# The first attention of a two-layer block: a head's rotations at other steps

## The reference

```python
h = (x - mu) * rsqrt(var + LN_EPS) * ln_scale + ln_bias
c_q = h @ w_down_q.T                       # 2048 x 64
c_kv = h @ w_down_kv.T
q = (c_q @ w_up_q.T)                       # 16 heads of 64
k = (c_kv @ w_up_k.T)
v = (c_kv @ w_up_v.T)
q = _apply_rope_subspace(q, DR)            # e*cos - o*sin, e*sin + o*cos
k = _apply_rope_subspace(k, DR)
attn = softmax(einsum('bhqd,bhkd->bhqk', q, k) / 8)
out = einsum('bhqk,bhkd->bhqd', attn, v) @ w_out.T + residual
```

## Time and profile before

| | us |
|---|---|
| median of 3 runs | 2236.38 (2236.3 to 2242.65) |
| the profiled execution | 2237.01 |
| its span | 2235.1 |
| PE busy in the span | 2009.0 (90%) |
| DVE, ACT, POOL busy | 1694.8, 1625.8, 1633.9 |
| attention, step 0 to the last output product | 61.4 to 1297.1 |

### The profile page before, as it was taken

How to read it: one execution, slowest core, us unless ns; L and a number is a source line. 1 busy time by engine, 2 the same in 40 slices (tenths; PEclk the granted TensorE clock), 3 DMA queues, 4 the chain that set the end, 5 groups by cost and what they waited for, 6 DMA issues and landing times. The chain is left out here.

```text
span 2235.1 us, 60603 instructions
## 1 busy us (share of the span) xinstructions
PE 2009.0 (90%) x24318; PEld 1317.7 (59%) x24318; DVE 1694.8 (76%) x3487; ACT 1625.8 (73%) x3282; POOL 1633.9 (73%) x1036
## 2 busy tenths in 40 slices
PE   5899999999999999999999979976678787887888
PEld 2466666666666666666666646642456666666665
DVE  5677777777778777777777558978988898899624
ACT  3798898988988988988889936656656555574543
POOL 4799998999999999989989936626664334577700
PEclk8899999999999999999999989977889999899769
DMA  4000100010000001000100000111211111121201
GB/s 151 22 23 16 30 23 16 23 29 18 23 23 23 23 19 27 23 16 23 30 16 23 2 16 23 40 36 25 41 41 48 34 43 36 32 46 36 43 10 38
DMA packets 88224, 67.80 MB, mean 30 GB/s; under 512 B 41280, under 2 KB 78352, under 8 KB 87952
## 3 DMA queue, kind: packets, MB, share of 16 engines
q1 hardware_dynamic: 76432, 52.19, 9.1%
q0 software_dynamic: 11520, 11.82, 2.6%
HBM read 32.97 MB, written 1.61 MB: 15 GB/s over the span
## 5 line engine op out<-in xcount | busy, mean ns | idle before, releaser
L428 POOL TENSOR_TENSOR probs_lo<-probs,probs_hi 128x1024 f16<-128x1024 f32 x512 | 1077.0, 2134 | 87.3 <-ACT probs L477 86.2
L533 DVE TENSOR_REDUCE part_max<-aux 128x1 f32<-128x512 f32 x1024 | 690.0, 688 | 210.9 <-PE aux L608 206.0
L476 ACT ACTIVATE probs_hi<-scores 128x512 f16<-128x512 f32 x1024 | 632.8, 618 | 162.7 <-PE scores L641 149.0
L477 ACT ACTIVATE probs<-scores 128x512 f32<-128x512 f32 x1024 | 638.7, 624 | 0.0
L1732 POOL DMA_INDIRECT far<-key_table,placeT x320 | 328.6, 1027 | 236.8 <-issue 70.1
L655 PE MATMUL acc<-v,probs_hi 128*128 128x65 f16 x4096 | 445.9, 193 | 1.8 <-POOL probs_lo L428 1.8
L657 PE MATMUL acc<-v,probs_hi 128*128 128x64 f16 x4096 | 446.9, 195 | 0.0
L659 PE MATMUL acc<-v,probs_lo 128*128 128x65 f16 x4096 | 445.2, 193 | 0.0
L655 PEld LDWEIGHTS acc<-v,probs_hi 128*128 128x128 f16 x4096 | 383.0, 97 | 72.1 <-POOL probs_lo L428 2.1
L608 PE MATMUL aux<-k_a,q_a 128*128 128x512 f16 x1024 | 394.4, 386 | 32.4 <-issue 22.9
L657 PEld LDWEIGHTS acc<-v,probs_hi 128*128 128x128 f16 x4096 | 380.8, 97 | 68.9 <-issue 0.6
(11 more groups left out here) (335 smaller groups left out, 3619.1 us busy)
## 6 DMA issues: line engine op xcount, KB each, us to landing
q_a<-rope_high SPq DMA_DIRECT2D x128, 64.0 KB, 2.0
far<-key_table,placeT POOLq DMA_INDIRECT x360, 2.5
q_b<-rope_low SPq DMA_DIRECT2D x64, 64.0 KB, 2.0
k_b<-rope_high SPq DMA_DIRECT2D x64, 64.0 KB, 2.0
k_a<-rope_high SPq DMA_DIRECT2D x64, 64.0 KB, 2.1
k_a<-rope_low SPq DMA_DIRECT2D x64, 64.0 KB, 2.0
qT<-qT SPq DMA_DIRECT2D x16, 256.0 KB
queries<-places SPq DMA_DIRECT2D x7, 512.0 KB, 3.7
```

The costliest lines, as they stand in the source:

```text
L428: pool.tensor_tensor(probs_lo[:, slot], probs[:, wide], probs_hi[:, slot], ALU.subtract).then_inc(low_ready, 1)
L476: act.activation(probs_hi[:, slot, i], bank, ACT.Exp, scale=float(DH0) ** -0.5)
L477: act.activation(probs[:, wide, i], bank, ACT.Exp, scale=float(DH0) ** -0.5).then_inc(probs_ready, 1)
L533: dve.tensor_reduce(part_max[g % 2][:, n % QT, n // QT:n // QT + 1], bank, AX.X, ALU.max).then_inc(aux_free, 1)
```

## The change

`rope_at` returns other steps for heads 1 to 15: the first query pair 27 steps ahead of its head instead of 17, the key pairs 21 and 15 steps ahead instead of 30 and 23, and the second query pair 5 instead of 4. Head 0 keeps its own steps. In a head's own counting the next head's rotations now lie in steps 5 (first query pair), 11 and 17 (keys), and 27 (second query pair). ACT's copies, POOL's subtractions and SP's transfers move with them, since their places are worked out from the same function.

```diff
 def rope_at(kind, h, pair):
 
     if kind == "k":
-        return STEPS * (h - 1) + (2, 9)[pair] if h else -24 + pair
-    return STEPS * h - (17, 4)[pair] if h else (-25, 0)[pair]
+        return STEPS * h - (21, 15)[pair] if h else -24 + pair
+    return STEPS * h - (27, 5)[pair] if h else (-25, 0)[pair]
```

## The result

The changed kernel takes **2217.5 us** (median of six runs, 2214.95 to 2221.07). The kernel before, run beside it, took 2237.92 (2235.35 to 2242.65). The ratio is **0.9902, 95% interval 0.9884 to 0.992**: about 1% faster, against a forecast of 2214.5 in a range of 2208 to 2224. The profiled execution has a span of 2216.5 us, 18.6 less than before.

What follows compares the result with a forecast made beforehand. PE was taken to pace the first attention, with removable waits for the first queries' transfers in step 19. Terms -25.2 + 1.3 + 2 = -21.9 us, from the median 2236.4, gave 2214.5 us, range 2208 to 2224.

Steps and rivals of the forecast that it cites:

- The waits of step 19: Heads 1 to 14, PE before the second maximum product: all 14 waits go, 21.8 us, -25.2 us with half clock.
- Half clock behind two of the waits: Heads 3 and 11: half-speed stretches following PE's waits disappear, saving 3.4 us.
- Keys' margin: Step 23, second key pair's low halves: they land 1.5 us early in even heads, 2.9 in odd; no cost.
- The slower rival: Step 23: keys' subtraction two low halves later on POOL, trip misses its reader, 28 us more, 2242.5 us; chance 0.05.
- POOL and DVE: Whole heads and step 5: no added PE waits; at most 0.8 us for POOL and 1.4 us for DVE.
- Head 0's shade: Head 0, step 3: head 1's first key rotation leaves step 2, so PE's wait grows by 1.3 us.
- The residual addition: Head 0, around POOL's 4.53 us addition: moved rotations cost +2 us, within -1 to +2.5.
- The rival that PE is not the pacer: First attention: POOL needs PE's pause, which returns as waits for probs_lo; nothing gained, 2236 us; chance 0.06.

Runs made afterwards that it cites:

- second profile: The changed kernel run again without further edits, on the chip of the last comparison: 2217.71 us, 0.9907 of the kernel before.

## Why the prediction was right, and where it was not

**The waits of step 19: right.** Forecast -25.2 us for heads 1 to 14, measured -24.64. The reading as the tail of a trip, too long by 1.4 us, is shown by the lead of one step more and one step less. Half clock behind two of the waits went with them: the granted clock of heads 1 to 14 is 1.00, and even and odd heads last 73.51 and 76.23 us (73.5 and 76.3 forecast). The prediction called these two the longer waits; the longest of all, 2.52 us in head 10, had a granted clock of 1.00 in the 6 us behind it, so their length does not tell the two apart.

**Whose move removes them: too narrow.** The prediction gave all of it to the first queries' rotation, and priced the keys' move only for what it could cost. That step reckoned the trip against PE's work of before, and left out that the change puts a rotation of 1.30 us into just that stretch. The first queries' move alone is enough, and the keys' move without it brings 19.4 of the 24.6 us. The sum wasn't hurt, since either way the wait goes.

**Keys' margin, taken at nothing: right, but not as safe as written.** At best 1.37 us against 1.5. That is less than the scatter of a landing (median 2.1, at most 3.6 us in the changed kernel and 4.0 with one step less). It shows in the changed kernel in a few steps only, such as the 0.3 us in its list of waits. The slower rival was a real mechanism: two steps later costs more than the whole gain. Its waits were priced about right for such a delay (28 us; 34.9 with the drain, two steps later), but it left out the half clock behind them, 14.0 us. Its trigger, POOL two low halves late, didn't come.

**POOL and DVE, taken at nothing: right for PE.** PE is idle for 0.36 us in 14 heads, though POOL is busy for 70.23 of 73.51 us in an even one. POOL does hold ACT up. ACT's waits for it in heads 1 to 14, before and after:

```profile
ACT probs_hi L476 <- POOL probs_lo L428: 9.0, 8, 1.3
```

```profile
ACT probs_hi L476 <- POOL probs_lo L428: 21.9, 27, 1.3
```

They lie in 13 of the 14 heads after the change. The prediction named waits of ACT for probs_lo in most heads as the sign that PE is not the pacer. The sign came and its case did not, since none of these waits reached PE. With the first queries' move alone they are 3.0 us, so it is the other rotations' places that bring them.

**Head 0's shade, +1.3: right in size**, 1.29 us by which step 3 grows; putting these keys back gave 0.82 us in the later steps. **The residual addition, +2: mis-sized.** Steps 6 to 31 of head 0 hold as many rotations as before and take 66.17 us against 65.56, +0.6, inside the bounds of -1 to +2.5, but near their middle. "POOL is busy without a gap" was no ground for the upper end. What is left of head 0's +2.30, 0.4 us, lies in its steps 3 and 4, at a granted clock of 0.77 and 0.54 against 1.00 and 0.57 before. It differs from one execution to the next: head 0 took 87.44 in the second profile.

**The rival that PE is not the pacer: fell.** In the kernel with the first queries' move alone PE is busy for 1048.72 of 1048.72 us, and the heads shortened by what its waits took. The Trainium skill (Perfetto Trace Analysis, Identifying the Most-Contended Engine) names two measures for TensorE in place of matmul busy time: MFU, the arithmetic done as a share of what the engine could do at its peak, and weight-load busy time. The second is 47.05 of 73.51 us here, or 64%, which would put PE behind POOL; the measurement disagrees with that ranking. MFU was not worked out.

**The 3 us between forecast and median.** Half of them are the base: the forecast starts from 2236.4 us, and the kernel before took 2237.92 beside the changed one, so the medians fell by 20.4 us against 21.9 forecast. In the profiled pair the part up to the end of the attention shortened by 23.2 us, more than forecast. The difference lies outside what the change touches, as far as the profiles show: behind the attention the same work took from 934.4 to 947.6 us in 13 profiled executions of all these kernels. That the sum came so near is thus partly luck. Why one execution gets more full clock there than another is open. The shortest, one step earlier for the first queries, and one near the longest, one step later for the keys:

```profile
1273.20:2207.60 934.40, 769.26 (x7838) 524.70 (x7838) 740.75 (x1890) 527.56 (x1120) 461.32 (x444) 0.88 0.16 35
```

```profile
1282.80:2230.10 947.30, 782.30 (x7838) 536.44 (x7838) 741.25 (x1890) 527.41 (x1120) 456.39 (x444) 0.86 0.16 35
```

## What to carry to other kernels

A wait for a transfer is its trip minus the work that the waiting engine has in between. It goes when the producer is issued earlier, and also when other work that is due anyway is put into the gap; reckon both against the schedule after the change. One step of lead was enough here; keep a margin over the scatter of landings, whose latest came 1.5 and 1.9 us behind the median here, and look at what work lost its place in the shade of another wait.

## What the runs showed of the hardware

Equal transfers of 64 KB into the keys' tile land after 1.9 to 3.6 or 4.0 us, median 2.1. SP's issuing stretches as well, rows here of its queue (start us, us, line): two issues that mostly take 1.10 us took 1.96, and four that mostly take 2.4 took 3.73. The first fence is of the kernel with keys one step later, the second of the changed kernel.

```profile
352.60 1.10 SPq L413 DMA_DIRECT2D k_a<-rope_low  x2
...
375.42 1.96 SPq L413 DMA_DIRECT2D q_b<-rope_low  x2
```

```profile
395.33 2.39 SPq L407 DMA_DIRECT2D q_a<-rope_high  x4
...
446.70 3.73 SPq L407 DMA_DIRECT2D q_a<-rope_high  x4
```

And a wait can cost more than its idle time on an engine that is otherwise busy throughout: 13 of 14 waits of some 3.3 us were followed by half clock, at 1.65 us each, where 12 of the 14 waits of before, 1.2 to 2.5 us, were not. The length alone does not decide it: waits of 1.76 and 1.83 us had it, and the one of 2.52 us did not.
